# Router products in fewer, wider matmuls, and the weight work of the first expert placed elsewhere on the vector engine

## The reference

```
mod = (silu(c) @ wmod)                    # shifts, scales and gates: sa ca ga sb cb gb per sequence
h = layernorm(x) * (1 + ca) + sa
q, kv, a = rmsnorm(h) @ w_qkva.T          # a through a sigmoid
x = x + ga * (q * scan(a, kv))            # s[t] = a[t] * s[t-1] + kv[t] along the sequence
h = layernorm(x) * (1 + cb) + sb
probs = softmax(h @ Wr)                   # 8 experts; each token goes to its two best
pos = how many earlier (token, choice) pairs of the batch row chose the same expert
keep = pos < capacity                     # 1024 / 8 * 1.25 tokens per row: later tokens are dropped
y = relu(buf @ W1[e] + b1[e]) @ W2[e] + b2[e]
x = x + gb * sum over the two choices of keep * prob * y
```

## Time and profile before

| | |
|---|---|
| time, median of 3 runs | 2215.82 us (2215.57 to 2216.04) |
| profiled execution: its time, its span | 2212.34 us, 2210.6 us |
| PE busy | 2167.0 us, 98% of the span |
| DVE busy | 1597.7 us, 72% |
| ACT busy | 1031.5 us, 47% |
| POOL busy | 362.2 us, 16% |
| mean granted TensorE clock | 0.995 of full speed |
| share of the chain that ended last | PE 91%, DVE 4%, all else 5% |

### The profile page before, as it was taken

One profiled execution on the slowest core, in us unless ns is written; L12 is line 12 of the kernel. 1 busy time (PEld: TensorE's weight loads), 2 busy tenths in 40 slices (PEclk: granted clock), 3 DMA queues, 4 the chain that ended last, 5 costly groups with the idle time before them and its releaser, 6 DMA issues.

```text
span 2210.6 us, 34370 instructions
## 1 busy us (share of the span) xinstructions
PE 2167.0 (98%) x12938; PEld 1196.2 (54%) x12938; DVE 1597.7 (72%) x2818; ACT 1031.5 (47%) x2042; POOL 362.2 (16%) x334
## 2 busy tenths in 40 slices
PE   7999999999999999999999999999999999999997
PEld 2445545545474746555564646556464655556463
DVE  6799989999785487587758758775875787487341
ACT  5456766657351436155344615433460644356050
POOL 0123343433323010101101010100101010100101
PEclk9999999999999999999999999999999999999999
DMA  7779997665675244344524543452345345343201
GB/s 271 240 209 256 225 256 181 155 174 135 144 201 156 78 123 137 94 115 111 150 71 104 143 111 98 124 156 72 96 134 120 105 124 144 85 102 96 44 6 24
DMA packets 350886, 296.78 MB, mean 134 GB/s; under 512 B 242331, under 2 KB 242331, under 8 KB 350208
## 3 DMA queue, kind: packets, MB, share of 16 engines
q1 hardware_dynamic: 328960, 252.44, 41.5%
q0 software_dynamic: 21760, 42.14, 10.0%
HBM read 159.64 MB, written 93.01 MB: 114 GB/s over the span
## 4 chain that ended last, share of the span: by engine, by line
PE 91%; DVE 4%; SPq 1%; DMA 1%; issue 1%; ACT 1%; POOL 0%; DVEq 0%; ACTq 0%; POOLq 0%
PE bank L1970 37%; PE bank L1911 28%; PE bank L1828 20%; PE bank L1899 4%; PE bank L1783 1%; PE bank L1794 1%; DVE wmx L1376 1%; PE bank L1739 0%; SPq L472 0%; DMA reg_d<-in_wmod 0%; DMA mod_rows<-reg_a 0%; DVE reg_c L1178 0%; DMA reg_e<-reg_e 0%; DVE reg_b L1435 0%; SPq L474 0%
## 5 line engine op out<-in xcount | busy, mean ns | idle before, releaser
L1970 PE MATMUL bank<-reg_b,reg_c 128*128 128x512 f16 x3840 | 831.7, 379 | 1.0 <-DVE reg_b L1435 1.0
L1970 PEld LDWEIGHTS bank<-reg_b,reg_c 128*128 128x128 f16 x3840 | 375.6, 98 | 452.0 <-issue 1.9
L1828 PE MATMUL bank<-reg_c 128*128 128x512 f16 x2304 | 509.4, 380 | 2.3 <-DMA reg_c<-reg_a 2.2
L1911 PE MATMUL bank<-reg_e,reg_a 128*128 128x320 f16 x2688 | 417.6, 299 | 0.0
L1828 PEld LDWEIGHTS bank<-reg_c 128*128 128x128 f16 x2304 | 223.3, 98 | 262.6 <-issue 5.9
L1911 PEld LDWEIGHTS bank<-reg_e,reg_a 128*128 128x128 f16 x2688 | 262.2, 98 | 105.2
L735 POOL DMA_INDIRECT out_dram<-reg_e,midx x80 | 140.1, 1751 | 1012.2 <-DVE reg_e L1457 901.3
L1453 DVE SCALAR_TENSOR_TENSOR reg_e<-bank,inv,reg_e 128x512 f32<-128x512 f32 x80 | 59.9, 748 | 263.6 <-PE bank L1970 263.6
L946 ACT ACTIVATE reg_e<-bank,b1s 128x320 f32<-128x320 f32 x112 | 59.1, 527 | 394.0 <-PE bank L1911 394.0
L1911 PE MATMUL bank<-reg_e,reg_d 128*128 128x320 f16 x1344 | 217.0, 299 | 0.0
L1911 PEld LDWEIGHTS bank<-reg_e,reg_d 128*128 128x128 f16 x1344 | 130.4, 98 | 53.8 <-ACT reg_e L946 3.8
(11 more groups left out here) (227 smaller groups left out, 2602.9 us busy)
## 6 DMA issues: line engine op xcount, KB each, us to landing
reg_d<-in_w SPq DMA_DIRECT2D x224, 512.0 KB, 4.3
slot_rows<-zrow SPq DMA_DIRECT2D x32, 516.0 KB, 4.9
reg_b<-in_x SPq DMA_DIRECT2D x16, 1024.0 KB, 6.9
out_dram<-reg_b SPq DMA_DIRECT2D x16, 1024.0 KB, 6.5
reg_d<-in_w SPq DMA_DIRECT2D x8, 1024.0 KB, 9.4
slot_rows<-zrow SPq DMA_DIRECT2D x32, 129.0 KB, 4.7
reg_d<-in_wmod SPq DMA_DIRECT2D x4, 1024.0 KB, 14.5
reg_e<-mod_rows SPq DMA_DIRECT2D x7, 512.0 KB, 4.4
```

The source lines that it names most:

```text
L1828: ins = mm(dst[:, :], wqs[:, ws, kc, e0:e0 + P], xns[:, j % 2, xs, kc, :], start=kc == 0 and xs == 0 and ws == 0, stop=kc == KC - 1 and ws ...
L1911: ins = mm(dst[:, 0:CAP], w[ws][:, c, p * P:(p + 1) * P], xs_of[:, KC * xs + 2 * i + c, j * CAP:(j + 1) * CAP], start=first and c == 0 and ...
L1970: ins = mm(bank_y[i % 2][:, :], hid[:, hs, hc, t * P:(t + 1) * P], w2s[:, ws, hc, :], start=k == 0 and hs == 0 and ws == 0, stop=k == HC - ...
```

## The change

Five edits, all in the stage of attention and in unit 0:

- **Logits.** The high half of h2 now meets both halves of the router weights in one matmul of 16 columns; the low half meets the high weights in one of 8. They leave two sums of 8 columns a tile in the bank, which DVE joins with a copy and an add into a new tile `lgs` (two more links in `route_choose`, so `NCH`, `NRT` and the counts in `exps` rise by two).
- **Positions.** One product for all four tiles where each tile had its own: 5 matmuls of 32, 24, 16, 8 and 32 columns in place of 14 of 8.
- **Maxima.** `w_max_quarter` once in each of the steps 1 to 4, ahead of the second half of `apply2`; what hangs on it moves from step 2 to step 4, and the high halves on ACT from steps 3 to 5 to steps 6 to 8.
- **Low halves in step 15.** The four `w_lo` stand in four places: behind `mix` 1, behind the second half of `apply2`, behind `mix` 2, and behind `mix` 3.
- **PE's wait.** In unit 0 the wait for all four low quarters becomes a wait for quarter kc + 1 where the low half of quarter kc is first used, in the first hidden group.

```diff
@@ route_choose (DVE)
-                raw = bank_r[:, 0:TB * E].rearrange("p (t e) -> p t e", t=TB)
+                both = bank_r[:, 0:2 * TB * E].rearrange("p (t s e) -> p t s e", t=TB, s=2)
+                raw = lgs[:, :, :]
                 wait(dve, s_lg, TB * n + TB)
+                lk(v_.tensor_copy(lgs[:, :, :], both[:, :, 1, :]))
+                lk(v_.tensor_tensor(lgs[:, :, :], both[:, :, 0, :], lgs[:, :, :], ALU.add))
                 lk(v_.tensor_reduce(rv[:, 0, :], raw, AX, ALU.max))
@@ step (DVE)
                 if has(i, 0):
                     mix(q, j, 1)
+                if i == 15:
+                    dve.wait_ge(s_xn, 16 * TB * NB)
+                    w_lo(0, 0, 0)
                 if has(i, -2):
                     route_place(oq, oj)
-                if i == 2:
-                    for c in (2, 3):
-                        w_max_quarter(0, 0, c)
+                if 1 <= i <= 4:
+                    w_max_quarter(0, 0, i - 1)
+                if i == 4:
                     w_scale_head(0, 0)
                 if has(i, -1):
                     apply2(pq, pj, 1)
                 if i == 15:
-                    dve.wait_ge(s_xn, 16 * TB * NB)
-                    w_lo(0, 0, 0)
                     w_lo(0, 0, 1)
                 if has(i, 0):
                     mix(q, j, 2)
                 if i == 15:
                     w_lo(0, 0, 2)
-                    w_lo(0, 0, 3)
-                if i == 2:
+                if i == 4:
                     pm_reduce()
                 if has(i, -1):
                     lo2(n - 1, pj)
                 if has(i, 0):
                     mix(q, j, 3)
+                if i == 15:
+                    w_lo(0, 0, 3)
...
-                if i == 1:
-                    for c in (0, 1):
-                        w_max_quarter(0, 0, c)
-                if i == 2:
+                if i == 4:
                     pm_copy()
                     w_scale_tail(0, 0, 7)
                     b1_scale(0)
@@ logits (PE)
-                for k, (xs, ws) in enumerate(((0, 0), (0, 1), (1, 0))):
-                    for c in range(KC):
-                        ins = mm(bank_r[:, t * E:(t + 1) * E], h2T[:, 4 * xs + c, t * P:(t + 1) * P], wrs[:, ws, c, :],
-                                 start=k == 0 and c == 0, stop=k == 2 and c == KC - 1)
+                o = bank_r[:, 2 * t * E:2 * (t + 1) * E]
+                for c in range(KC):
+                    mm(o, h2T[:, c, t * P:(t + 1) * P], wrs[:, :, c, :], start=c == 0, stop=False)
+                for c in range(KC):
+                    ins = mm(o[:, 0:E], h2T[:, KC + c, t * P:(t + 1) * P], wrs[:, 0, c, :], start=False, stop=c == KC - 1)
@@ positions (PE)
-                for t in range(TB):
-                    o = bank_r[:, 64 + t * E:64 + (t + 1) * E]
-                    mm(o, upper[:, :], mh[:, t, :], start=True, stop=False)
-                    for k in range(t):
-                        mm(o, ones[:, :], mh[:, k, :], start=False, stop=False)
-                    ins = mm(o, ones[:, :], cm[:, :], start=False, stop=True)
+                o = bank_r[:, 64:64 + TB * E].rearrange("p (t e) -> p t e", t=TB)
+                mm(o, upper[:, :], mh[:, :, :], start=True, stop=False)
+                for k in range(TB - 1):
+                    mm(o[:, k + 1:, :], ones[:, :], mh[:, k:k + 1, :].to_broadcast([P, TB - 1 - k, E]), start=False, stop=False)
+                ins = mm(o, ones[:, :], cm[:, :].unsqueeze(1).to_broadcast([P, TB, E]), start=False, stop=True)
@@ plain_unit (PE)
-                pe.wait_ge(s_wlo, 4)
                 pe.wait_ge(s_xt, 16 * (u + 1))
...
+                                if u == 0 and hb == 0 and ws == 1 and b == 0:
+                                    wait(pe, s_wlo, kc + 1)
```

More of the change, by code:

```diff
@@ L44 @@
 MODW = 6 * D + 8
-NCH = 12
-NRT = 26
+NCH = 14
+NRT = 28
 XSCALE = 16.0
@@ L215, in build_program @@
         lim = sb("lim", [P, E], F32)
+        lgs = sb("lgs", [P, TB, E], F32)
         dlg = sb("dlg", [P, TB, E], F32)
@@ L804, in exps @@
                 r0 = rt_at(n // 4, n % 4)
-                wait(act, s_rt, r0 + 2)
+                wait(act, s_rt, r0 + 4)
                 a.activation(prb[:, :, :], dlg[:, :, :], ACT.Exp, scale=ir[:, 0:1]).then_inc(s_ex, 1)
-                wait(act, s_rt, r0 + 7)
+                wait(act, s_rt, r0 + 9)
                 a.activation(ex2[:, :], rv[:, 2, :], ACT.Exp, scale=ir[:, 0:1]).then_inc(s_ex, 1)
@@ L880, in step @@
                     stats1(*rel(q, j, 2))
-                if 3 <= i <= 5:
-                    w_hi_quarter(0, 0, i - 3)
+                if 6 <= i <= 8:
+                    w_hi_quarter(0, 0, i - 6)
                 if i == 14:
@@ L1848, in step @@
                         turn_gate()
-                    if i == 2 and k == 9:
+                    if i == 4 and k == 9:
                         pe.wait_ge(s_wch, 7)
                         tr(bank[7][0:1, 384:512], wmx[:, 5:6], ident32[:, :]).then_inc(s_pmt, 1)
-                    if i == 2 and k == 11:
+                    if i == 4 and k == 11:
                         pe.wait_ge(s_pm, 1)
```

## The result

The changed kernel takes 2201.03 us (median of 4, 2197.33 to 2202.80) against 2215.70 beside it: a ratio of 0.9932, 95% interval 0.9915 to 0.9949. Forecast were 2201.3 and a range of 2198.0 to 2206.5. The profiled execution took 2202.21 us, its span is 2200.5, PE is busy for 2157.7 us (98%) where it was 2167.0.

The account below looks back on a forecast made before the run. PE, busy for 98% of the span, was taken to bound the kernel. The terms 8.75 - 0.8 + 5.8 + 0.6 + 0.2 = 14.5 us came off a median of 2215.8, giving 2201.3 us, range 2198.0 to 2206.5.

Parts of the forecast that it names:

- Products: Logits and positions on PE: 25 fewer small matmuls a block at 25 ns, over 14 blocks, gain 8.75 us.
- The serial reading: Logit and position matmuls on PE: if wider columns add to the 25 ns, the products give 7.6 us.
- One thing has no slack: Logits waiting for SP's transposes: later scatters cost 0.15 us in five of thirteen steps, -0.8 us, bounds 0 and -2.
- Maxima: Steps 2 to 5: one maximum a step regains 5.8 of 8.7 us lost, bounds 3 and 7.5.
- Rival (a): Steps 3 and 4: the maxima only shift their wait, giving 2 to 3 us; time 2205 to 2207; chance 0.22.
- Unit 0: Start of unit 0: PE's wait moves behind 22 matmuls, 3.3 us long, at half clock; gain 0.6 us.
- The lower clock follows a wait of this length: Start of unit 0: half clock behind the 3.3 us wait loses about 1.65 us in the turns.
- rival (b): Unit 0's wait doesn't cost the clock, or transposes behind free DMA engines don't wait: 2198 to 2200 us; chance 0.12.
- Blocks 14 and 15: Unit 0: block 14 gives 0.625 us on PE, block 15's two links add 0.45; together +0.2 us.
- Carrying the trace to the median: Whole kernel: the profiled run's time lay 3.5 us below the median; this difference was carried over to the median, 2215.8.
- waits of the logits in steady steps: Sign against the forecast: it would be wrong if steady steps showed PE waiting at the logits.
- the turns of over 2.5 us at unit 0: Sign for the forecast: behind PE's 3.3 us wait at unit 0 the turns take over 2.5 us.

Follow-up runs that it names:

- e12: The changed kernel run again unaltered, a third time, beside other follow-up runs: 2201.73 us.
- e10: The changed kernel without the join of the two logit sums, DVE reading only one, so 12 links again: 2198.32 us.
- e4: The changed kernel with the load of the next x held back until the transposes of h have landed: 2201.13 us, ratio 0.9935.
- e2: The kernel before with only the first maxima, what hangs on them and the high halves moved: 2209.07 us, ratio 0.9971.
- e3: The kernel before with only the four low quarters of step 15 spread and PE's wait taken per quarter: 2212.80 us, ratio 0.9989.
- e1: The kernel before with only the router's products changed (logits, positions and join): 2206.36 us, ratio 0.9962.
- e6: The changed kernel without its unit 0 part: low quarters where they stood before, one wait for all four: 2200.17 us.
- e5: The changed kernel with the scale of the first W1 moved from step 4 to step 5, the maxima staying: 2198.63 us.
- e8: The changed kernel run again unaltered, a second time: 2199.34 us.
- e11: The kernel before run again unaltered: one run, 2214.66 us.
- e7: The changed kernel with the last turns (block 15) put ahead of PE's wait for the fourth low quarter: 2198.89 us.

## Why the prediction was right, point by point

The total was right within 0.3 us, with terms off that offset each other. Measured is the mean of three traces of the changed kernel against the mean of two of before; where other kernels have the same code in a stretch, their traces are added and named.

- **Products, 8.75 us.** Right: 0.63 us in each of 14 steps, 25 ns at 16 columns and 26 at up to 32. The serial reading (7.6) is out. The Trainium skill, "TensorE: Matmul & The Clock Gate", section Back-to-back issue gap, gives a floor of about 25 ns for matmuls of 1 to 64 columns. The trace agrees with it beyond the 8 columns that before could show, up to 32.
- **"One thing has no slack", -0.8 us.** Right mechanism, too small: steps 6 to 15 lose 1.9 to 3.9 us (mean 3.2) against 0.1 and 0.9 of before, so -2.8, outside the bounds of 0 and -2. It took the wait to stand in one step of before, where it stands in three (0.12 to 0.14 us at steps 8, 12 and 15), and had `route_place` and its scatters 0.4 us later; in step 11 of e12 the first scatter is 1.0 and the last 1.3 later, partly because POOL hands lateness on. That the two links are the cause is shown by e10, in one trace, and by the traces without them (0.06 to 0.85 us lost); that it goes by way of the scatters is the likely reading and no more. It is not the load of x (e4).
- **Maxima, 5.8 us.** 8.1 less 3.7 is 4.3, inside the bounds of 3 and 7.5. The head of step 2 is clean as forecast, and step 5 shows 0.64 + 1.40 = 2.04 where the text had 1.4 (1.8 with the tiny products). Alone (e2) the maxima give 5.3 to 6.6; what is missing comes only where the products stand beside them. With e3's 11.05 the mean of before is 9.1, and the term 5.3. Rival (a) would have left 5.7 to 6.7 us lost in these steps; 3.3 to 4.1 are.
- **Unit 0, 0.6 us.** Between the last attention matmul and the turns' end it is 11.4 before and 8.7 after, 2.7 us; with e1, e2 and e6 on one side and e3, e4, e5 and e10 on the other it is 11.2 and 9.2, 2.0 us. The place and length of the wait (22 matmuls, then 3.3 forecast, 3.35 measured) were right. "The lower clock follows a wait of this length" was not a rule: it followed in e8, e3, e4 and e5 (turns of 2.58 to 3.62 us) and not in the profile after, e12 or e10 (1.91), and before's own 10.74 is 12.05 in its second trace. So the first half of rival (b) came true in three traces of seven; its second did not. What the part is worth in the time is open: 3.4 us on top of before (e3), 0.8 on top of the rest (e6), both near the edge of what the runs can tell.
- **Blocks 14 and 15, +0.2 us.** 55.0 before and 55.05 after on the mean, but before's two traces are 52.9 and 57.1, as far apart as the term of the maxima is large. With e2 and e3 (57.62, 57.18) the mean of before is 56.2 and the term a gain of 1.1 us; e1, the products alone, has 54.66. What gives it was not looked into.
- **Carrying the trace to the median.** Before's first trace had a stretch of 52.89 us that e11 and two kernels with the same code there don't repeat, so adding its distance to the median was right. Still, part of the agreement within 0.3 us is luck: the terms measured sum to 8.8 - 2.8 + 4.3 + 2.7 = 13.0 us on the few traces and to 8.8 - 2.8 + 5.3 + 2.0 + 1.1 = 14.4 on all, while the medians differ by 14.7 (16.1 and 14.3 in the other groups). The -0.8 that should have been -2.8 was made good by unit 0 and block 15, which gave some 2 us more than forecast.

What would have shown it wrong was named: waits of the logits in steady steps. They are there, in one to five steps of a trace of the changed kernel, but not in the number that would cost more than the products give. Of the signs that it would be right, the turns of over 2.5 us at unit 0 failed in two of three traces; the others came.

## What to carry to other kernels

Small matmuls cost their issue pace, 25 ns here from 8 to 32 columns, so making them wider and fewer is free until some other engine must pay for it: here the price of the wider logits was two links of 0.22 us on DVE, and they cost more than their length, with scatters that more often end late beside the transposes that PE waits for. When a step has 1 us of slack on one engine, look for a second engine that hands the lateness on, as POOL does here behind its scatters. One-time work that makes a full step late can move to the next step (e5). A wait that can't be removed can be filled: look for the next work on the waiting engine that doesn't need what is waited for (e7, seen in its trace and not in the medians).

## What the runs showed of the hardware

The length of a wait alone doesn't decide the granted clock behind it. In steady work 48 matmuls of 512 columns take 10.52 us, behind the 1.71 us wait 12.21, and some 3.4 us at half clock cost 1.7. The half clock came behind the 3.94 us ahead of unit 0 in all five traces that have this wait, behind the 3.1 to 3.4 us there in four of seven, behind the 2.77 us of step 2 in one of four, and behind waits of 1.71 (the changed kernel, step 11) and 1.76 us (e3, step 4) at the logits.

In thirteen of fourteen traces, all but the first of before, PE stops at or just ahead of the logits of block 15 for over 1.1 us in all with nothing to wait for, and goes on in bits that are mostly 0.7 us apart. The timeline of PE in e12:

```profile
638.19 0.17 PE L1797 MATMUL bank<-wrs,reg_e 128*128 128x16 f16 x1
638.90 0.17 PE L1797 MATMUL bank<-wrs,reg_e 128*128 128x16 f16 x1 [0.54 <-issue]
639.62 0.21 PE L1797 MATMUL bank<-wrs,reg_e 128*128 128x16 f16 x2 [0.55 <-issue]
```

In e11 it adds 1.1 us to the logits, and behind the positions PE waits 2.11 us for ACT, where the first trace of before waited for next to nothing (0.08); that is most of the difference between 52.9 and 57.1 us. DVE and ACT start nothing in these moments either. In four of the thirteen (the profile after, e2, e3, e10) the half clock follows; the matmuls behind these logits in the profile after and then in before:

```profile
639.99 11.62 PE L1903 MATMUL bank<-reg_e,reg_a 128*128 128x320 f16 x72
```

```profile
651.99 9.94 PE L1899 MATMUL bank<-reg_e,reg_a 128*128 128x320 f16 x72
```

The standstill falls where eight scatters and four transposes have just been issued. What stops the engines was not found.
